# Four K slots and eight Q slots instead of two and four in an eight-core attention kernel

## The reference, cut to what matters

```python
def _L0_attn_ref(x, Wq, bq, Wk, bk, Wv, bv):        # x: (4, 2048, 4096), float32
    q = (x @ Wq.T + bq)                             # 32 heads of 128
    k = (x @ Wk.T + bk); v = (x @ Wv.T + bv)        # 16 heads of 128
    scores = jnp.einsum('bgkqd,bkld->bgkql', q, k) * SCALE
    scores = jnp.where(causal, scores, jnp.float32(-jnp.inf))
    w = jax.nn.softmax(scores, axis=-1)
    return jnp.einsum('bgkql,bkld->bgkqd', w, v)    # laid out again as (4, 2048, 4096)

def _L0_ffn_ref(x, base_W, router_W, lora_A, lora_B):
    base = x @ base_W.T
    w_dense = ...                                   # top 2 of 8 experts, from softmax(x @ router_W.T)
    mid = jnp.einsum('bsd,edr->bser', x, lora_A) * w_dense[..., None]
    return base + jnp.einsum('bser,erd->bsd', mid, lora_B) * SCALING

xn = _layernorm(x)
out = x + _L0_attn_ref(xn, ...) * _silu(_L0_ffn_ref(xn, ...))
```

## Time and profile before

| | us |
|---|---|
| runs of the kernel before, median | 2271.85 |
| profiled execution, slowest core | 2279.68 |
| its span, core 4 | 2277.8 |
| spans of the other cores | 2257.6 to 2275.2 |
| span of core 6 | 2263.2 |
| core 4: TensorE matmul busy | 1853.3 (81%) |
| core 4: weight loads, ACT, DVE, GpSimd busy | 1160.7, 547.9, 311.4, 93.6 |
| core 4, mean granted TensorE clock | 0.918 |

### The profile page before, as it was taken

How to read it: one execution, slowest core, us unless ns; L and a number is a source line. 1 busy time by engine, 2 the same in 40 slices (tenths; PEclk the granted TensorE clock), 3 DMA queues, 4 the chain that set the end, 5 groups by cost and what they waited for, 6 DMA issues and landing times.

```text
span 2277.8 us, 32519 instructions; the slowest of 8 cores (2257.6 to 2277.8 us)
## 1 busy us (share of the span) xinstructions
PE 1853.3 (81%) x12788; PEld 1160.7 (51%) x12788; DVE 311.4 (14%) x897; ACT 547.9 (24%) x647; POOL 93.6 (4%) x92
## 2 busy tenths in 40 slices
PE   1054329999999999999999899999999556687883
PEld 0011104444444444448887588888888323444442
DVE  0002680000000000000000000000000263534223
ACT  0054000100010001000100011111011346788993
POOL 1011000000000000000000000000000000000000
PEclk7589559999999999999999999999999768999997
DMA  9999003555444444442350344444441366645325
GB/s 153 163 165 147 2 0 41 61 59 62 59 56 58 56 56 56 58 66 37 55 83 17 46 67 75 72 76 75 73 75 41 81 146 130 141 127 125 93 80 93
DMA packets 230999, 177.96 MB, mean 78 GB/s; under 512 B 123587, under 2 KB 219076, under 8 KB 226372
## 3 DMA queue, kind: packets, MB, share of 16 engines
q0 software_dynamic: 155408, 85.53, 31.8%
q1 hardware_dynamic: 73140, 73.57, 12.9%
q10 hardware_dynamic: 2304, 16.78, 2.1%
HBM read 194.27 MB, written 67.11 MB: 115 GB/s over the span
## 4 chain that ended last, share of the span: by engine, by line
PE 69%; DMA 8%; DVE 7%; ACT 5%; another core or an unknown queue 5%; issue 4%; DVEq 0%; SPq 0%; POOL 0%; ACTq 0%; POOLq 0%
PE psB L343 10%; PE psA L343 10%; PE pg L343 10%; PE pg L558 7%; PE psB L558 6%; PE psA L558 6%; ACT arena L759 5%; DMA arena<-xT 4%; PE psA L479 3%; PE pg L479 3%; PE psB L479 3%; DMA wstr<-Qs 3%; PE pav L666 2%; DVE arena L298 2%
## 5 line engine op out<-in xcount | busy, mean ns | idle before, releaser
L343 PE MATMUL pg<-arena,wstr 128*128 128x512 bf16 x1024 | 238.0, 389 | 68.5 <-DVE arena L301 68.5
L343 PE MATMUL psA<-arena,wstr 128*128 128x512 bf16 x1024 | 223.6, 379 | 0.0
L343 PE MATMUL psB<-arena,wstr 128*128 128x512 bf16 x1024 | 223.6, 379 | 0.0
L343 PEld LDWEIGHTS pg<-arena,wstr 128*128 128x128 bf16 x1024 | 101.0, 99 | 204.0 <-issue 88.6
L759 ACT ACTIVATE arena<-psA,konst 128x1024 bf16<-128x1024 f32 x160 | 178.1, 1113 | 96.7 <-PE psA L752 94.2
L759 ACT ACTIVATE arena<-psB,konst 128x1024 bf16<-128x1024 f32 x160 | 177.8, 1111 | 8.4 <-PE psB L752 6.7
L558 PE MATMUL pg<-wstr,arena 128*128 128x256 bf16 x1408 | 161.7, 275 | 11.5 <-DMA wstr<-bwT 11.5
L752 PE MATMUL psA<-wstr 128*128 128x512 bf16 x320 | 104.5, 411 | 77.5 <-DMA wstr<-Qs 47.7
L343 PEld LDWEIGHTS psB<-arena,wstr 128*128 128x128 bf16 x1024 | 100.2, 98 | 120.8
L343 PEld LDWEIGHTS psA<-arena,wstr 128*128 128x128 bf16 x1024 | 100.2, 98 | 120.8
L558 PEld LDWEIGHTS pg<-wstr,arena 128*128 128x128 bf16 x1408 | 138.6, 98 | 29.0 <-issue 12.0
(11 more groups left out here) (114 smaller groups left out, 1389.0 us busy)
## 6 DMA issues: line engine op xcount, KB each, us to landing
arena<-xT POOLq DMA_DIRECT2D x32, 512.0 KB, 24.5
wstr<-wqT POOLq DMA_DIRECT2D x16, 1024.0 KB, 13.6
wstr<-bwT POOLq DMA_DIRECT2D x8, 2048.0 KB, 21.4
gH<-vsb SPq DMA_DIRECT2D x128, 128.0 KB, 2.2
arena<-gH ACTq DMA_DIRECT2D x16, 1024.0 KB, 5.6
out<-arena POOLq DMA_DIRECT2D x16, 1024.0 KB, 15.7
Qs<-vsb SPq DMA_DIRECT2D x64, 128.0 KB, 2.5
wstr<-wkT POOLq DMA_DIRECT2D x8, 1024.0 KB, 13.3
```

Source lines behind the costliest of these rows:

```text
L343: em.emit("T", lambda E, pp=pp, sl=sl, ch=ch, ts=ts: nc.tensor.matmul(pp[:, :], wbuf[sl][:, ch * 128:(ch + 1) * 128], xnT[:, ch * T + ts * ...
```

## The change

It doubles the slots for K and for Q, placing the new ones in columns of `wstr` that phase D did not use, and issues the loads for head u+4 instead of u+2 at step u. Before the loop it issues those of heads 0 to 3. The sizes and the number of the loads stay.

```diff
-        q_slot = [wstr[:, 4096 + 512 * i: 4096 + 512 * (i + 1)] for i in range(4)]
-        k_slot = [wstr[:, 0:2048], wstr[:, 2048:4096]]
+        q_slot = ([wstr[:, 4096 + 512 * i: 4096 + 512 * (i + 1)] for i in range(4)]
+                  + [wstr[:, 10240 + 512 * i: 10240 + 512 * (i + 1)] for i in range(4)])
+        k_slot = [wstr[:, 0:2048], wstr[:, 2048:4096],
+                  wstr[:, 6144:8192], wstr[:, 8192:10240]]
...
             def emit_k(qsx, i):
-                ksl = i % 2
+                ksl = i % 4
...
-                qsl = (qsx * 16 + uu) % 4
+                qsl = (qsx * 16 + uu) % 8
...
-            kuse = {0: 0, 1: 0}
-            quse = {0: 0, 1: 0, 2: 0, 3: 0}
+            kuse = {i: 0 for i in range(4)}
+            quse = {i: 0 for i in range(8)}
...
                 if qs == 0:
-                    emit_k(0, 0)
-                    emit_q(0, 0)
-                    emit_q(0, 1)
+                    for _w in range(4):
+                        emit_kq_ahead(0, _w)
...
-                        ksl = i % 2
-                        emit_kq_ahead(qs, u + 2)
+                        ksl = i % 4
+                        emit_kq_ahead(qs, u + 4)
```

## The result

| | before | after |
|---|---|---|
| median of 8 runs each, us | 2273.09 | 2245.35 |
| ratio | | 0.9877, 95% interval 0.9861 to 0.9894 |
| profiled execution, slowest core's span | 2277.8 (core 4) | 2244.8 (core 2) |
| span of core 4 in it | 2277.8 | 2242.9 |

The change takes 1.2% off, 28 us in the median. That is within the 2% to which the forecast gave 0.96, and the interval leaves no change out. A few of the runs were disturbed and lie far above the rest; the ratio leaves them out.

What follows compares the result with a forecast made beforehand. Waits, chiefly for Q loads, were taken to bound the first three quarters. Removing 33 us took the profiled 2279.7 to 2246.7; the median's 7.8 us allowed 2238.9, and the middle, 2243, was forecast, range 2232 to 2262.

Steps and rivals of the forecast that it cites:

- The lead: K issue to first reader, early second quarter: grows from 5.3 to 23.5 us, above the worst landing of 15.6.
- The worth, by steps: First three quarters at undisturbed step lengths: at most 6.8, 21.8 and 5.6 us go, together 34.2, taken as 33.
- The first wait: Start of the attention phase: the 15.4 us wait stays, and six more queued loads cost nothing.
- SP's order: SP's queue: same load instructions; the mid-quarter V loads come two steps sooner and are read only next quarter.
- part 1 of the working: K and Q slots: four K slots release each K four steps earlier, eight Q slots follow; lead becomes 23.5 us.
- The clock: TensorE after load waits: matmuls partly at 1.2 GHz; the step count already holds this, and the first quarter's terms stay.
- more than the waits: Rival at quarters' first steps: denser work holds 2.4 GHz, saving 1.8 us twice; time 2235, chance 0.08.
- The median: Whole run: median lies 7.8 us under the profiled run; 2243 is the middle of 2246.7 and 2238.9.
- the upper end: Whole run: if the 7.8 us lay in core 4's load waits, 25.2 us remain to lose and time is 2246.7.
- bandwidth: Rival in the second quarter: busier DMA engines keep half or all of its gain; time 2254 or 2265, chance 0.17.
- The short lead: Rival at the Q waits: lead was never short, 128 KB lands in 2.3 us, DVE's mask decides; 2272, chance 0.05.
- Late gate rows: Slower rival at quarter ends: moved loads delay the last 1 MB gate load; time up to 2314, chance 0.03.

Runs made afterwards that it cites:

- e4: Changed kernel with three K and six Q slots instead of four and eight; ratio 0.9885 to the kernel before.
- e8: Changed kernel with the first K and two Qs issued ahead of the four V loads at the attention phase's start; ratio 0.9836 to the kernel before.
- e1: Changed kernel with the doubled slots but the old issue distance, head u+2 at step u; ratio 0.986 to the kernel before.
- e12: Changed kernel with first K and Q ahead of V, deferred multiplies, no wait for zero, one reciprocal wait dropped, later V loads on GpSimd; ratio 0.9798 to before.
- e9: Changed kernel with each quarter's gate multiplies halved and spread over steps 1 to 8 of the next quarter, stores following; ratio 0.9859 to before.
- e5: Kernel before the change without the output stores of the first three quarters and the waits on their semaphores; ratio 0.9877 to the kernel before.
- e1 to e4: Four slot variants of the changed kernel: old issue distance 0.986, K slots only 0.9895, Q slots only 0.9957, three K and six Q slots 0.9885.
- e11: Changed kernel without the scaling's always-met wait for zero on earlier stores in the first two quarters; ratio 0.9853 to the kernel before.

## Why the prediction was right

The time is 2245.4 where 2243 was forecast.

1. *The lead.* It was given as 5.3 us before and 23.5 after in the second quarter, and for e4 as 14.4. The changed kernel measured 23.5 and e4 14.35. The bound to hold it against was too low: I took 15.6, the worst landing before, and after the change the loads that meet the stores land in 20.2 us on core 2 and in 21.4 on core 7. The forecast held by 2 to 5 us and not by 8; that it held was in part luck. (The 17.9 us of the earlier trace rows is mostly of the stores at the end of the second quarter; the four of the first end landed in 10.3 to 24.5 us. Nothing in the sum used it.)
2. *The worth, by steps.* 6.8, 21.8 and 5.6 us were the upper ends on core 4, 33 taken. Core 4's quarters by the masks fell from 61.6, 91.9 and 103.7 to 56.0, 70.6 and 98.8, by 5.6, 21.3 and 4.9, which is 31.8. Its span fell by 34.9; the first mask came 2.8 us earlier, which is no work of the change. To count by steps was the right choice. That the sum of the waits, 32.3, came out the same was not the confirmation that I took it for: in core 4's 45 steps the Q waits fell by 32.3 us, DVE's mask took back 8.1 (29.5 to 37.6), and TensorE was busy 9.8 less (184.8 to 175.0) at a clock of 0.80, 0.96 and 0.97 instead of 0.69, 0.86 and 0.94. Two terms that the waits leave out nearly cancel.
3. *The first wait* stayed, 14.7 us. Six more loads queued there cost it nothing. That it must stay was wrong: "the loads still start only when the base projection has released the buffer" is true of K and Q, but they stood behind V loads that wait for the last gate store as well, and e8 took half of it.
4. *SP's order.* The V loads did come earlier and hurt nothing. e1 shows that the distance of four heads is no part of the gain, as part 1 of the working implies, though the text did not say so.
5. *The clock.* The granted clock of the second quarter rose from 0.87 to 0.96 and of the first from 0.67 to 0.77. In the first it gave nothing beyond the waits: its steps are 3.64 us at either level. The quarters' first steps stayed slow (6.5 and 9.3 us), so the rival of more than the waits fell. Its mechanism is real where the idle time at the end is shorter: in e12 the second quarter's first step is 4.5 to 4.6 us at a granted clock of 1.00 on six cores, and 5.1 and 5.3 us at 0.75 and 0.70 on the other two.
6. *The median.* The middle between 2246.7 and 2238.9 was a guess at where 7.8 us of the profiled run lay. After the change the cores span 2233.9 to 2244.8 where they spanned 2257.6 to 2277.8: what set core 4 apart was its load waits, and the upper end was the right one. Core 4 did not stay the longest, as the sum had it: core 2 is, by 1.9 us.

The rivals: bandwidth kept nothing. The second quarter ran its DMA engines at 0.73 and 169 GB/s, close to the 0.77 and 167 worked out, and still hid it. e9 and e12 show that this rival is real a step further on. The short lead was real: TensorE waits for usual loads in e5 as well, where no landing exceeds 8.6 us, 3.6 us in quarter 2. These loads take 4.1 us in the median. The Trainium skill's fit (DMA: Bandwidth & Descriptors, Anatomy of one DMA) is stated for transfers that GpSimd issues and gives 2.3 us by my estimate. SP issues these, and the measured 4.1 us decides. The rival itself falls by e1 to e4: the slots took the waits away. Late gate rows did not appear; they land in 7.1 us against 6.4.

The fourth quarter was forecast as unchanged. Its 15 steps vary between 139.9 and 144.4 us over cores and kernels, at the first step (9.7 to 12.6) and at one further step (mostly 9.3 or 10.6), and took 1.3 us off the gain in the mean of the cores (141.8 before, 143.1 after). The clock goes with it. Three first steps, of core 1 before the change and of cores 1 and 4 after it:

```profile
2083.82:2093.51 9.69, 6.94 (x72) 4.39 (x72) 2.70 (x13) 6.76 (x7) 0.86 (x1) 1.00 1.07 181
```

```profile
2055.35:2066.69 11.34, 8.59 (x72) 5.70 (x72) 2.71 (x13) 6.79 (x7) 0.86 (x1) 0.85 1.07 197
```

```profile
2061.93:2074.24 12.31, 9.53 (x72) 6.33 (x72) 2.71 (x13) 6.77 (x7) 0.86 (x1) 0.73 1.05 177
```

The same 72 matmuls take 6.94, 8.59 and 9.53 us at a granted clock of 1.00, 0.85 and 0.73, and the step is longer by what they take. The further step is 10.6 us at 0.85. In e9, with less idle time at the quarter ends, the first step is 9.7 us at 1.00 and the quarter 139.9 to 140.0 us on every core. Open: why one core falls to the lower clock there and another does not. No run tests that.

## What to carry to other kernels

Compare the lead of a load, from the release of its slot to its first reader, with the landing time of the worst load that the slot will meet, not with the median; more slots buy lead in whole steps, and a K that waits for its slot holds back everything behind it in the queue. The distance at which the program lists a load is no lead on a queue that runs on its own. Price what a wait costs by the length of undisturbed steps and not by the wait: here another engine took over a part of the waits removed, and the matmuls ran at a higher clock without them.

## What the hardware showed that I had not expected

A wait that is always met is not free: 0.06 to 0.07 us on DVE between a reciprocal and the scaling that reads it, 4.4 us of a quarter in which DVE sets the step (e11). It does not cost that everywhere: of four such waits of the reciprocals in a step, one cost 0.07 us (e12). A queue can be held by issuing alone: four loads of 256 KB, in pieces of 256 bytes, took SP 31 us while accumulating stores and gate loads ran (e9), 12 to 17 us shortly behind the stores (e1) and 3 to 9 us in the kernels before and after the change.
